# The first and the last iterations of a pipelined graph-network kernel written out by hand, engine by engine

## The chip, the cores and the metric

The kernel runs on 1 core of one Trainium2 chip. The metric is the device time of one execution in microseconds (us); lower is better. The time before is the median of 3 runs.

## The reference

128 graphs of 128 nodes, 256 features each, pass through four layers; after each one the layer's result is added to its input and the row is normalised. All of it is float32.

```python
H = (adj != 0);  w = adj[:, 0, :]
# L0: two hypergraph convolutions, relu and layer norm between them
xw = x @ W1.T;  Dn = 1 / (H @ w);  Be = 1 / H.sum(axis=1)
h = relu(Dn * (H @ (Be * (H.T @ xw))) + b1)
h = layer_norm(h) * gamma + beta
y = Dn * (H @ (Be * (H.T @ (h @ W2.T)))) + b2 + x
x = norm(x + y)                                                   # n1 -> x1
# L1: mean aggregation
x = norm(x + relu(concat([x, adj @ x / max(adj.sum(-1), 1e-6)]) @ W.T))   # n2 -> x2
# L2: three graph convolutions
g = relu(adj @ (x @ V1) + c1);  g = relu(adj @ (g @ V2) + c2)
x = norm(x + adj @ (g @ V3) + c3)                                 # n3 -> x3
# L3: one convolution, with rows masked that are zero throughout
out = relu((adj @ x) @ K) * (any(x != 0))
x = norm(x + out)                                                 # n4 -> x4
```

## The kernel before, in words

Two graphs make a pair, and there are 64 pairs. The work of a pair is cut into 17 stages on TensorE (PE); `LAG` gives the iteration, counted from the pair's own number, in which each stage runs: G (H times its weighted transpose), Tr (a transpose), Gx in iteration p; R, P, GP in p+1; xT, XAB, AXB in p+2; Ax2, H1, H1W, H2 in p+3; H2W, AP3, Ax3, TK in p+4; the last sum, n4, in p+5. Iteration n so works on five or six pairs at once, and PE runs the stages in the order R G xT H2W Ax2 XAB H1 AP3 P Tr AXB H1W Ax3 Gx H2 GP TK. A product of precision is made of three matmuls, high by high, high by low and low by high: the tiles `*_hi` are rounded copies, made on ScalarE (ACT), and the tiles `*_lo` are the rest, made by a subtraction on VectorE (DVE) where the source lies in PSUM, and on GpSimd (POOL) where it lies in SBUF: `low_r` (r_lo), `low_p` (p_lo), h1 and h2 (both h_lo), `low_GT`, `low_A`.

Each engine has a program of its own, `fill()` and then `body(n)`, and runs it strictly in order; semaphores tie them together. `fill()` holds iterations 0 to 2 and the preparation of the weights: `w2_columns` and `betaW_rows` are two small PE products (psum<-w2g,ones and psum<-n_s,beta_b), from which DVE makes the centred `w2c_hi`, `w2c_lo` and `betaW`. From iteration 3 on `body(n)` is the same to the last iteration, 68, with those stages left out that have no pair (`if active(...)`). Where a stage writes in the 8 PSUM banks is fixed by `BANK`; a stage waits until the one before it in its bank has been read.

The end of a pair (iteration p+5, stage F): ACT takes the relu of TK's product (L846, tk), DVE counts the non-zero elements of x3 (L1151, L1155: mask), POOL multiplies tk by mask (L1321) and adds x3 (L1329: n4.s), DVE takes the moments, ACT the root, DVE the inverse and the shift (L888), ACT writes x4 (L576), and SP stores it.

In the rows matmuls and their tiles are named as the program names them: psum<-gx,w1T is R, psum<-w2c,r is P, psum<-p,GT is GP, psum<-ident,x is xT, psum<-wab,x1T is XAB, psum<-xbw,A is AXB, psum<-A_f,x is Ax2 or Ax3, psum<-ax,v is H1, psum<-v,h is H1W or H2W, psum<-A_f,h1w is H2, psum<-h2w,A is AP3, psum<-wk,ax is TK.

Of the kernel before, what the change touches and what calls it, by code (L numbers as in the profile page):

```python
# [16 lines left out]
LAG = dict(prep=-1, G=0, Tr=0, Gx=0,  # L17
           R=1, P=1, GP=1,
           x1=2, xT=2, XAB=2, AXB=2,
           x2=3, Ax2=3, H1=3, H1W=3, H2=3,  # L20
           H2W=4, AP3=4, Ax3=4, TK=4,
           F=5)


BANK = dict(R=0, Ax2=0, Tr=0, GP=4, H1=1, Gx=1, XAB=2, AXB=2, TK=2, H2=3, xT=4, P=4,
            H2W=6, H1W=6, G=(5, 7), AP3=7, Ax3=7)
# [4 lines left out]
def build(nc, x, adjT, w1T, w2T, wab, v1, v2, v3, wk, columns, rows, eye, out):
# [4 lines left out]
    END = NP + LAG["F"]  # L36

    with ExitStack() as ctx:
# [133 lines left out]
        def first(n, j):  # L172

            return n == j

        def active(stage, n):
            return 0 <= n - LAG[stage] < NP

        def bank(stage, pair):

            if stage == "G" and pair == 2:
                return 6, 7
            if stage == "Tr" and pair in (1, 2):
                return 3 * pair
            if stage == "GP" and pair == 0:
                return 2
            if stage == "xT" and pair == 0:
                return 3
            return BANK[stage]

        def steps(fill, body):

            fill()
            for n in range(FILL, END):
                body(n, n)

        def at_count(p, k):
# [1196 lines left out]
```

## Time and profile before

| | |
|---|---|
| time, median of 3 runs | 1439.89 us (1439.43 to 1441.12) |
| the profiled execution: its own time | 1440.07 us |
| its span, first to last instruction | 1438.3 us |
| PE busy | 1389.8 us, 97% of the span |
| DVE, ACT, POOL busy | 1119.3, 1124.9, 1045.4 us (78%, 78%, 73%) |
| chain of work that ended last | PE 94% |
| mean granted TensorE clock | 0.987 |

The profiled execution lies 0.18 us over the median, and its span 1.77 us under its own time. The busy time of PE counts a matmul from its start to its modelled end; in a row of matmuls without a gap they overlap, and what one costs is the distance from its start to the next one's.

### The profile page before, as it was taken

What the parts mean: (1) busy time and instruction counts of PE and PEld (TensorE: products, weight loads), DVE (VectorE), ACT (ScalarE), POOL (GpSimd) and SP (SyncE); (2) the same over time, 40 slices, a digit from 0 to 9 for tenths busy, and PEclk for the clock granted to TensorE, in tenths of its full rate; (3) what the DMA queues carried; (4) which work ended last, traced back from release to release, by engine and by line L of the source; (5) the groups of instructions that cost most, each with busy time, mean ns of one, the idle gap of its engine ahead of it and who ended that gap; (6) DMA issues with size and microseconds to landing.
All of it is one profiled execution on the core that took longest, in us unless ns stands there. A gap on an engine that the chain in (4) does not pass through costs nothing.

```text
span 1438.3 us, 34672 instructions
## 1 busy us (share of the span) xinstructions
PE 1389.8 (97%) x10896; PEld 1347.0 (94%) x10896; DVE 1119.3 (78%) x4060; ACT 1124.9 (78%) x2634; POOL 1045.4 (73%) x1096
## 2 busy tenths in 40 slices
PE   5899999999999999999999999999999999999974
PEld 5799999999999999999999999999999999999974
DVE  5578888887877878878878888787787787887763
ACT  4578788788788778878878878878877877887853
POOL 4667777877877877777787787787787777777742
PEclk9899999999999999999999999999999999999997
DMA  3001011011011011011101101101101101100000
GB/s 128 22 24 38 19 39 38 20 39 38 20 38 38 20 38 38 27 31 38 33 25 39 38 20 38 38 20 38 39 20 38 39 20 38 39 29 18 16 15 23
DMA packets 29956, 47.13 MB, mean 33 GB/s; under 512 B 3408, under 2 KB 12240, under 8 KB 29776
## 3 DMA queue, kind: packets, MB, share of 16 engines
q1 hardware_dynamic: 29776, 44.91, 10.0%
q8 instruction: 90, 1.47, 0.4%
q14 instruction: 90, 0.74, 0.2%
HBM read 28.12 MB, written 16.78 MB: 31 GB/s over the span
## 4 chain that ended last, share of the span: by engine, by line
PE 94%; DVE 2%; issue 1%; ACT 1%; POOL 0%; DMA 0%; POOLq 0%; ACTq 0%; DVEq 0%
PE psum L265 91%; PE psum L384 2%; PE psum L313 1%; DVE n_st L866 1%; DVE p_f L1009 0%; ACT x L576 0%; DVE n_s L1039 0%; DVE n_s L1178 0%; DVE psum L1029 0%; DMA at_in<-adjT 0%; ACT n_std L571 0%; DVE x L898 0%; DVE w2g L1095 0%; ACT h_f L581 0%; DVE psum L871 0%
## 5 line engine op out<-in xcount | busy, mean ns | idle before, releaser
L576 ACT ACTIVATE x<-n_s,n_shift,n_rstd 128x256 f32<-128x256 f32 x384 | 208.8, 592 | 1.2 <-DVE n_shift L888 0.9
L1229 POOL TENSOR_TENSOR h_lo<-h_f,h_hi 128x512 fp32r<-128x512 f32 x128 | 164.1, 1282 | 55.4 <-ACT h_hi L557 55.4
L1237 POOL TENSOR_TENSOR r_lo<-r_f,r_hi 128x512 fp32r<-128x512 f32 x128 | 164.6, 1288 | 52.7 <-ACT r_hi L557 45.9
L1321 POOL TENSOR_TENSOR n_s<-tk,mask 128x512 f32<-128x512 f32 x64 | 66.7, 1042 | 154.8 <-DVE mask L1155 141.3
L265 PE MATMUL psum<-v_hi,h_hi 128*128 128x256 f32 x512 | 150.5, 294 | 5.8 <-issue 4.5
L866 DVE BATCH_NORM_STATS2 n_st<-n_s 128x6 f32<-128x256 f32 x384 | 141.9, 411 | 7.5 <-POOL n_s L1329 5.2
L265 PE MATMUL psum<-w2c_hi,r_hi 128*128 128x258 f32 x512 | 147.2, 287 | 0.0
L265 PE MATMUL psum<-w2c_lo,r_hi 128*128 128x258 f32 x512 | 145.9, 285 | 0.0
L265 PE MATMUL psum<-v_hi,h_lo 128*128 128x256 f32 x512 | 145.2, 284 | 0.0
L265 PE MATMUL psum<-w2c_hi,r_lo 128*128 128x258 f32 x512 | 145.1, 283 | 0.0
L265 PE MATMUL psum<-v_lo,h_hi 128*128 128x256 f32 x512 | 144.9, 283 | 0.0
L265 PE MATMUL psum<-gx_hi,w1T_hi 128*128 128x256 f32 x512 | 144.3, 282 | 0.0
L265 PE MATMUL psum<-A_f,x 128*128 128x128 f32 x1024 | 138.8, 280 | 5.2 <-ACT x L576 4.4
L265 PE MATMUL psum<-gx_hi,w1T_lo 128*128 128x256 f32 x512 | 143.7, 281 | 0.0
L265 PE MATMUL psum<-gx_lo,w1T_hi 128*128 128x256 f32 x512 | 143.6, 280 | 0.0
L581 ACT ACTIVATE h_f<-psum,columns 128x256 f32<-128x256 f32 x256 | 107.3, 471 | 44.9 <-PE psum L265 44.9
L571 ACT ACTIVATE n_std<-psum,eps_c 128x2 f32<-128x2 f32 x192 | 49.2, 256 | 116.8 <-DVE psum L871 116.8
L265 PEld LDWEIGHTS psum<-A_f,x 128*128 128x128 f32 x1024 | 128.4, 196 | 5.8 <-ACT x L576 4.8
L1229 POOL TENSOR_TENSOR p_lo<-p_f,p_hi 128x512 fp32r<-128x512 f32 x64 | 81.9, 1280 | 63.9 <-ACT p_hi L557 63.9
L855 DVE TENSOR_TENSOR ax_lo<-psum,ax_hi 128x512 fp32r<-128x512 f32 x128 | 88.6, 692 | 33.7 <-ACT ax_hi L557 29.5
L855 DVE TENSOR_TENSOR x1T_lo<-psum,x1T_hi 128x512 fp32r<-128x512 f32 x64 | 44.3, 692 | 81.8 <-ACT x1T_hi L557 81.8
L265 PE MATMUL psum<-wab_hi,x1T_hi 128*128 128x512 f32 x256 | 107.5, 420 | 0.0
(158 smaller groups left out, 5426.2 us busy)
## 6 DMA issues: line engine op xcount, KB each, us to landing
x_in<-x_in_dram SPq DMA_DIRECT2D x64, 256.0 KB, 2.8
out<-x SPq DMA_DIRECT2D x64, 256.0 KB, 2.0
at_in<-adjT SPq DMA_DIRECT2D x64, 128.0 KB, 2.2
x<-v_in SPq DMA_DIRECT2D x3, 256.0 KB, 5.1
n_s<-w2T_in SPq DMA_DIRECT2D x2, 256.0 KB, 3.8
r_f<-w1T_in SPq DMA_DIRECT2D x2, 256.0 KB, 4.7
h_f<-wab_in SPq DMA_DIRECT2D x2, 256.0 KB, 5.9
rows<-rows_in SPq DMA_DIRECT2D x1, 256.0 KB, 6.2
```

The costliest lines, as they stand in the source:

```text
L265: return pe.matmul(o, a, b, start=start, stop=stop)
L313: last = pe.transpose(psum[:, bank("Tr", p), cols(g)], Gd[:, g, :], ident[:])
L384: last = pe.transpose(psum[:, bank("xT", p), (2 * m + g) * C:(2 * m + g + 1) * C], x1[:, g, cols(m)], ident[:])
L571: act.activation(nm.std[:], nm.mv[:, :, 1], ACT.Sqrt, bias=eps_c[:, 0:1]).then_inc(nm.rooted, 1)
L576: last = act.activation(dst[:, g, :], nm.s[:, g, :], ACT.Identity, scale=nm.rstd[:, g:g + 1], bias=nm.shift[:, g:g + 1])
L581: return act.activation(dst[:, m].rearrange("p g c -> p (g c)"), psum[:, BANK[stage] + extra, (m % 2) * 2 * C:(m % 2 + 1) * 2 * C], ACT.Re ...
L855: return dve.tensor_tensor(dst[1][:], src, f(dst[0][:]), ALU.subtract).then_inc(signal, 1)
L866: last = dve.bn_stats(nm.st[:, g, :], sum_n1_psum(p, g) if nm is n1 else nm.s[:, g, :])
L1229: return pool.tensor_tensor(dst[1][:], src, f(dst[0][:]), ALU.subtract).then_inc(signal, 1)
L1237: pool.tensor_tensor(r_s[1][:, half], r_f[:, half], f(r_s[0][:, half]), ALU.subtract).then_inc(r_lo[h], 1)
L1321: pool.tensor_tensor(n4.s[:], tk[:], bc(mask[:], [C, 2, D], 2), ALU.mult).then_inc(tk_masked, 1)
```

## The change

The diff rewrites every engine's program. The functions of single steps (`R`, `low_gx`, `invert`, and so on) keep their instructions and take the pair's number alone. What differs:

1. Iterations 0 to 5 (`fill()`) and 63 to 68 (`drain()`) are lists of steps in an order of their own for each engine. The iterations in between, 6 to 62, keep the order that they had on every engine.
2. In these lists a stage may write in any bank: `BANK_OF` gives it, and the waits that keep a bank from being overwritten stand in the lists. R is split in its halves `R0` and `R1`, P in `P(p, 0)`, `P(p, 1)` and `squares(p)`.
3. In the lists a step of SBUF sources (`low_r`, `low_p`, `low_A`, `low_h1`, `low_h2`, `low_v`, `low_w1`, `low_wab`, `add_squares`, `sum_squares`, `make_xb`, `sum_n4`) may run on DVE or POOL. In fill 14 of POOL's steps stand on DVE and 3 of DVE's on POOL; in drain 16 of POOL's stand on DVE.
4. For pairs 60 to 63 (`MASKED`) the mask is the scale of the relu on ACT, one instruction for each graph, and `sum_n4` adds tk and x3 in one instruction. The multiplication on POOL is gone for them.
5. x1 has two buffers; the moments of n2, n3 and n4 lie in SBUF outside the middle iterations; the order of the loads is the one before, and each of the late weights has a semaphore of its own.
6. In the middle iterations the waits differ a little: PE has 55 in an iteration instead of 54, DVE 72 instead of 63, ACT 69 instead of 65, POOL 31 instead of 25.

```diff
+BANK_OF = {
+    ('G', 0): (6, 7), ('BW', 0): 0, ('Tr', 0): 1, ('Gx', 0): 2, ('W2', 0): 3, ('R0', 0): 4, ('G', 1): (6, 7),
...
+FIRST, LAST = 6, 63
+MASKED = 60
...
+        def sum_n4(e, p):
+            if p >= MASKED:
+                e.wait_ge(tk_relu, upto(p))
+                e.wait_ge(n4.done, upto(p - 1))
+                e.tensor_tensor(n4.s[:], tk[:], x3[:], ALU.add).then_inc(n4.summed, 1)
...
+            def fill():
+                G(0)
+                betaW_rows()
+                Tr(0)
+                Gx(0)
+                w2_columns()
+                R(0, 0)
+                pe.wait_ge(gd_made, 1)
+                G(1)
+                R(0, 1)
...
+                pe.wait_ge(w2_mean, 1)
+                P(0, 0)
+                pe.wait_ge(r_relu[0], 1)
+                pe.wait_ge(r_relu[1], 1)
+                G(2)
+                pe.wait_ge(gd_made, 2)
+                R(1, 0)
+                P(0, 1)
+                squares(0)
+                Tr(2)
...
+                R(1, 1)
...
+                Gx(2)
...
+                G(3)
+                pe.wait_ge(p_made, 1)
+                P(1, 0)
+                Tr(3)
+                P(1, 1)
+                squares(1)
+                pe.wait_ge(r_relu[1], 2)
+                GP(0)
...
+                H1(1)
+                AP3(0)
+                pe.wait_ge(h2_relu, 1)
+                H1W(1)
+                pe.wait_ge(ax2_lo, 2)
+                Ax3(0)
+                pe.wait_ge(n2.summed, 3)
+                H2(1)
+                TK(0)
...
+                AXB(63)
+                pe.wait_ge(h1_relu, 62)
+                H2(61)
+                pe.wait_ge(ax3_lo, 60)
+                H1(62)
+                pe.wait_ge(h2w_lo, 61)
+                TK(59)
+                pe.wait_ge(ax2_lo, 63)
+                H2W(61)
+                pe.wait_ge(h1w_out, 62)
+                H1W(62)
+                pe.wait_ge(n3.summed, 61)
+                Ax2(63)
...
+                H2(63)
+                pe.wait_ge(ax3_lo, 61)
+                AP3(62)
+                pe.wait_ge(h2_relu, 63)
+                TK(61)
+                pe.wait_ge(h1_relu, 64)
+                H2W(63)
+                pe.wait_ge(tk_relu, 61)
+                Ax3(62)
+                pe.wait_ge(h2w_lo, 63)
+                AP3(63)
+                pe.wait_ge(h1w_out, 64)
+                TK(62)
+                pe.wait_ge(ax3_lo, 62)
+                Ax3(63)
+                pe.wait_ge(n3.summed, 63)
+                TK(63)
...
+                    act.wait_ge(mask_made, upto(p))
+                    for g in range(2):
+                        last = act.activation(tk[:, g, :], psum[:, b, g * D:(g + 1) * D], ACT.Relu,
+                                              scale=mask[:, g:g + 1])
```

The start of PE's program before; the rows from gx on are R of pair 0:

```order
L265 MATMUL psum<-BH,HT 128x258 x2
L313 MATMUL psum<-ident,Gd 128x128 x2
L265 MATMUL psum<-GT,x_in 128x128 x4
L265 MATMUL psum<-w2g,ones 128x256 x4
L265 MATMUL psum<-gx_hi,w1T_hi 128x256
```

The same place of the change:

```order
L366 MATMUL psum<-BH,HT 128x258 x2
L366 MATMUL psum<-n_s,beta_b 128x256 x4
L406 MATMUL psum<-ident,Gd 128x128 x2
L366 MATMUL psum<-GT,x_in 128x128 x4
L366 MATMUL psum<-w2g,ones 128x256 x4
L366 MATMUL psum<-gx_hi,w1T_hi 128x256
```

The product for `betaW` (n_s is the buffer that w2T is loaded in) now stands between G and Tr of pair 0; before it followed P of pair 0.

POOL before, at the first p_lo, for whose end PE's GP of pair 0 waits; the BH rows are `make_BH` of pair 2:

```order
L1254 TENSOR_TENSOR BH<-at_in,BH 128x2
L1257 TENSOR_TENSOR be_rest<-be_inv,be_r 128x2
L1260 TENSOR_TENSOR BH<-HT,be_r 128x2x128
L1262 TENSOR_TENSOR BH<-HT,be_rest 128x2x128
L1285 TENSOR_TENSOR xb<-x_in,b2half 128x512
L1229 TENSOR_TENSOR p_lo<-p_f,p_hi 128x512
L1229 TENSOR_TENSOR GT_lo<-GT,GT_hi 128x256
```

POOL in the change, at the same p_lo:

```order
L202 TENSOR_TENSOR v_lo<-x,v_hi 128x512
L202 TENSOR_TENSOR wk_lo<-tk,wk_hi 128x512
L209 TENSOR_TENSOR r_lo<-r_f,r_hi 128x512
L202 TENSOR_TENSOR p_lo<-p_f,p_hi 128x512
L1860 TENSOR_TENSOR BH<-at_in,BH 128x2
```

xb, BH of pair 2 and GT_lo of pairs 0 and 1 no longer stand in front of or behind it; the low part of r of pair 1 (its second half) does, and the weights' low parts.

The end of DVE's program in the change; x is x3, tk the relu's result. In the program before no row n_s<-tk,x stood on DVE; POOL had n_s<-tk,mask and n_s<-n_s,x:

```order
L1448 TENSOR_SCALAR mask<-nz_count 128x2
L1391 RECIPROCAL n_rstd<-n_std 128x2
L1395 SCALAR_TENSOR_TENSOR n_shift<-n_mv,n_rstd 128x2
L202 TENSOR_TENSOR ax_lo<-psum,ax_hi 128x512
L254 TENSOR_TENSOR n_s<-tk,x 128x512
L1371 BN_STATS n_st<-n_s 128x6 x2
```

The sum of the last pair is one instruction on DVE, directly ahead of the moments that need it.

## Rows read from the trace of the kernel before

**Rows 1.** The page's head: the span, and PE's busy time.

```profile
span 1438.3 us, 34672 instructions
PE 1389.8 (97%) x10896; PEld 1347.0 (94%) x10896; DVE 1119.3 (78%) x4060; ACT 1124.9 (78%) x2634; POOL 1045.4 (73%) x1096
```

**Rows 2.** Windows: length; busy time (instructions) of each engine; granted clock; DMA share; GB/s.

```profile
0.00:97.05 97.05, 75.72 (x492) 69.69 (x493) 60.83 (x194) 52.24 (x125) 57.76 (x71) 0.93 0.20 64
17.72:54.86 37.14, 28.38 (x174) 25.89 (x172) 22.50 (x67) 17.34 (x43) 23.23 (x26) 0.86 0.08 22
97.05:118.38 21.33, 21.33 (x173) 20.77 (x171) 17.27 (x64) 16.81 (x40) 16.22 (x18) 1.00 0.00 1
118.38:1334.38 1216.00, 1216.00 (x9692) 1184.32 (x9691) 984.75 (x3593) 995.12 (x2338) 925.13 (x970) 1.00 0.11 32
1334.38:1438.30 103.92, 76.74 (x546) 72.19 (x544) 56.45 (x213) 60.69 (x133) 46.28 (x40) 0.88 0.05 19
1396.94:1438.30 41.36, 19.19 (x116) 17.60 (x116) 13.73 (x59) 16.41 (x35) 11.94 (x10) 0.75 0.07 26
```

**Rows 3.** Timeline of PE: start, duration; matmuls in a row without a gap.

```profile
1350.72 0.28 PE L265 MATMUL psum<-v_hi,h_lo 128*128 128x256 f32 x1
1350.83 1.05 PE L265 MATMUL psum<-A_f,x 128*128 128x128 f32 x8
1351.72 0.50 PE L265 MATMUL psum<-GT,x_in 128*128 128x128 f32 x3
...
1362.23 0.39 PE L265 MATMUL psum<-wab_lo,x1T_hi 128*128 128x512 f32 x1
1362.46 0.40 PE L265 MATMUL psum<-wab_hi,x1T_lo 128*128 128x512 f32 x1
```

**Rows 4.** Timeline of PE in the fill; in brackets the idle time ahead of the instruction.

```profile
5.65 0.80 PE L265 MATMUL psum<-BH,HT 128*128 128x258 f32 x2 [5.65 <-POOL BH L1262]
8.50 0.66 PE L313 MATMUL psum<-ident,Gd 128*128 128x128 f32 x2 [2.04 <-DVE Gd L945]
...
35.98 0.55 PE L265 MATMUL psum<-p_hi,GT_hi 128*128 128x256 f32 x1 [4.41 <-issue]
...
57.70 0.66 PE L384 MATMUL psum<-ident,x 128*128 128x128 f32 x4 [2.60 <-DVE x L898]
```

**Rows 5.** Timeline of DVE and POOL: the same POOL operation with and without DVE's.

```profile
15.55 1.49 DVE L1095 TENSOR_TENSOR w2g<-w2g,w2mean 128x1024 f32<-128x1024 f32 x1
...
15.92 1.72 POOL L1229 TENSOR_TENSOR GT_lo<-GT,GT_hi 128x256 fp32r<-128x256 f32 x1
35.84 0.72 POOL L1229 TENSOR_TENSOR GT_lo<-GT,GT_hi 128x256 fp32r<-128x256 f32 x1
```

**Rows 6.** Timeline of the last iterations: what PE waited for.

```profile
1414.96 0.36 PE L265 MATMUL psum<-v_hi,h_hi 128*128 128x256 f32 x1 [0.79 <-issue]
1418.09 0.36 PE L265 MATMUL psum<-h2w_hi,A_hi 128*128 128x256 f32 x1 [1.46 <-ACT h2w_hi L557]
1423.20 2.08 PE L265 MATMUL psum<-A_f,x 128*128 128x128 f32 x8 [4.16 <-ACT x L576]
```

**Rows 7.** Timeline of ACT, POOL and DVE behind the last matmul.

```profile
1429.68 0.60 ACT L846 ACTIVATE tk<-psum 128x512 f32<-128x512 f32 x1 [2.79 <-PE psum L265]
...
1430.35 1.04 POOL L1321 TENSOR_TENSOR n_s<-tk,mask 128x512 f32<-128x512 f32 x1 [12.93 <-ACT tk L846]
1431.47 1.26 POOL L1329 TENSOR_TENSOR n_s<-n_s,x 128x512 f32<-128x512 f32 x1
...
1432.76 0.75 DVE L866 BATCH_NORM_STATS2 n_st<-n_s 128x6 f32<-128x256 f32 x2 [5.25 <-POOL n_s L1329]
```

**Rows 8.** The page's groups: busy us, mean ns of one, idle before.

```profile
L1229 POOL TENSOR_TENSOR h_lo<-h_f,h_hi 128x512 fp32r<-128x512 f32 x128 | 164.1, 1282 | 55.4 <-ACT h_hi L557 55.4
...
L581 ACT ACTIVATE h_f<-psum,columns 128x256 f32<-128x256 f32 x256 | 107.3, 471 | 44.9 <-PE psum L265 44.9
...
L855 DVE TENSOR_TENSOR x1T_lo<-psum,x1T_hi 128x512 fp32r<-128x512 f32 x64 | 44.3, 692 | 81.8 <-ACT x1T_hi L557 81.8
```

More of the change, by code:

```diff
@@ L14 @@
 TINY = 1.1754944e-38
[L17 to L26, printed above, removed]
-BANKS = 8
-FILL = 3
+BANK = dict(R0=1, R1=0, Ax2=0, Tr=0, GP=4, H1=1, Gx=1, XAB=2, AXB=2, TK=2, H2=3, xT=4, P=4,
+            H2W=6, H1W=6, G=(5, 7), AP3=7, Ax3=7, W2=2, BW=3)
+BANKS = 8
+BANK_OF = {
[14 rows of a table added]
+}
+FIRST, LAST = 6, 63
+MASKED = 60
 def build(nc, x, adjT, w1T, w2T, wab, v1, v2, v3, wk, columns, rows, eye, out):
@@ L170, in upto, with inputs @@
             return min(pair, NP - 1) + 1
[L172 to L177, printed above, removed]
         def bank(stage, pair):
[L181 to L197, printed above, removed]
+            return BANK_OF.get((stage, pair), BANK[stage])
+        def inputs(p):
             return 16 * (p // RING + 1)
@@ L256, in _, with body @@
+                load_v(3)
+                load_at(3)
+                load_x(3)
+                reload(4)
+                reload(5)
+                reload(6)
+                reload(7)
+                store(0)
+            def body(n):
+                if n + 2 < NP:
+                    reload(n + 2)
+                store(n - 5)
+            fill()
+            for n in range(FIRST, NP + 5):
+                body(n)
             for j in range(2):
@@ L360, in P, with squares @@
+                last.then_inc(pe_did[f"R{h}"], 1)
+            def P(p, h):
+                if p == 0 and h == 0:
+                    pe.wait_ge(w2c_lo, 1)
+                pe.wait_ge(r_lo[h], upto(p))
+                for g in range(2):
+                    product(psum[:, bank("P", p) + g, 0:D + 2],
+                            [(part(r_s, ALL, m, g), part(w2c_s, ALL, m)) for m in (2 * h, 2 * h + 1)],
+                            start=h == 0, stop=h == 1)
+            def squares(p):
                 pe.wait_ge(sq_sum, upto(p))
@@ L554, in _ @@
+            fill()
+            for n in range(FIRST, LAST):
+                body(n)
+            drain()
         @block.scalar
@@ L639, in round_p, with high_x1T, high_h2w, high_ax2 @@
+            def high_x1T(p):
+                high("xT", x1T, x1T_hi, p, pe_did["XAB"])
+            def high_h2w(p):
+                high("H2W", h2w, h2w_hi, p, pe_did["AP3"])
+            def high_ax2(p):
+                high("Ax2", ax2, ax2_hi, p, pe_did["H1"])
+            def high_ax3(p):
+                high("Ax3", ax3, ax3_hi, p, pe_did["TK"])
+            def round_p(p):
                 act.wait_ge(p_made, upto(p))
@@ L1223, in _ @@
-            steps(fill, body)
+                prep(0)
+                spread_beta()
+                scale_G(0)
+                scale_w2()
+                prep(1)
+                copy_betaW()
+                low_w1(dve, 1)
+                low_gx(0)
+                halve_b2()
+                mean_w2()
+                make_xb(dve, 0)
+                centre_w2()
+                prep(2)
+                scale_G(1)
+                low_w2()
+                low_r(dve, 0, 1)
+                add_squares(dve, 0)
@@ L1354 @@
+            fill()
+            for n in range(FIRST, LAST):
+                body(n)
+            drain()
 def kernel(x, adj, L0_gnn_W1, L0_gnn_b1, L0_gnn_gamma, L0_gnn_beta, L0_gnn_W2, L0_gnn_b2, L1_gnn_W,
```

2041 lines of the change are left out of this document (1264 added, 777 removed), and 13 rows, old and new, of the table BANK_OF.

## The prediction

> **What bounds the kernel now.** I read the page's head first: PE is busy for 1389.8 of 1438.3 us, the other engines for 73 to 78% [rows 1]. Then the windows, to see where PE is not busy. Iterations 6 to 62 fill 118.38 to 1334.38 us; PE is busy for all of it at full clock, so an iteration costs 1216.00 / 57 = 21.33 us and nothing but matmuls sets it [rows 2]. All loss lies outside. A pair's matmuls are one iteration's, so 64 pairs need 64 x 21.33 = 1365.3 us, and the two weight products about 3.2 (an estimate: 8 float32 matmuls of 256 columns, each twice the 0.22 that one of 128 costs below). That makes 1368.5; the span is 1438.3; 69.8 us are lost.
>
> To split them, I need the work left at 1334.38, where iteration 63 begins. The distance between starts in the timeline is 0.12 us for a matmul of 256 columns, 0.23 for 512, and 0.89 for four float32 matmuls of 128 columns (1350.83 to 1351.72; the trace counts each as two) [rows 3]. By these R costs 2.84, P 3.23, XAB 2.89, each of H1, H1W, H2W, TK 1.40 to 1.52, AP3, AXB, GP about 0.78, Ax2, Ax3, Gx, H2 about 0.87, xT 0.36, G 0.24, Tr 0.17, together 21.33. Left over at 1334.38 are G, Tr, Gx of one pair, R, P, GP of two, xT, XAB, AXB of three, Ax2, H1, H1W, H2 of four, H2W, AP3, Ax3, TK of five: 68.1 us of work, which take 103.9 to the end. **The drain loses 35.8.** The rest, 34.0, is lost in the fill, before iteration 5 starts at 97.05 (63.1 us of work in 97.05). In both stretches the granted clock is also down: 0.86 in 17.72 to 54.86, 0.75 behind 1396.94 [rows 2]; the low of the two levels is 1.2 GHz, and it follows stretches in which PE stood idle.
>
> What PE waits for is latency: one pair's chain, with nothing else in PE's queue that may run. In the fill these are the first G (5.65), Gd (2.04), p_lo (4.41, a wait for POOL under the name of issue, since p_lo stands behind the BH and xb work there) and x1 (2.60) [rows 4].
>
> **The change part by part.** The middle is untouched: same order, 57 iterations, 57 x 21.33. PE gets one more wait in an iteration, DVE nine. PE now stands before 54 waits an iteration and still shows no gap [rows 2], so the waits of semaphores long reached cost it nothing; DVE has 21.33 - 17.27 = 4.1 us idle in an iteration, which covers nine waits unless each costs 0.45. I take 0, and up to 0.05 us an iteration (3 us) for the range.
>
> *Fill.* I followed the new lists by hand, each step with its duration from the trace and the waits that the code names.
> - Up to 22 us little can be won. w2c_lo, which P of pair 0 needs, hangs on a chain of loads, gx, W2's product, centring on DVE. betaW's product, now ahead of Tr of pair 0, waits for w2T and takes Tr from 8.50 to about 10.3, but it also brings the full clock earlier, and it is gone from behind P(0). R(0) starts at 14.5 (before 14.61), P(0) at 22.3 (22.16).
> - From there on R, G, Gx and P of pairs 1 to 3 stand between. P(0) ends at 28.4, GP(0) at 36.3 with P(1), G(2), G(3), Gx(2) done: 5.0 us of work more and 1.3 us earlier than before, so 6.3 ahead. The 4.41 wait is filled.
> - DVE then sets the pace for a while. XAB(0) ends at 46.1, AXB(0) at 51.6 (waits for xbw_lo), H1(0) at 62.8, Ax2(1) at 70.5. Small stalls follow for pair 1's h1_lo (2.3), x3(0) and h1w (0.8). TK(0) ends at 83.6, where R(4) starts, which is 97.05 before: 13.4 ahead.
> - Such a list is too smooth; each dip of PE's clock costs, as the 37 us at 0.86 before did. I take off 1.4: **12.0**.
>
> *Drain.* The work without any stall puts H2 of pair 63 (behind which 9.8 us of work stand) at 1334.38 + 68.1 - 9.8 = 1392.7. By hand the stalls are 0.75 (low_r of pair 62, since DVE runs 2 us behind), 0.5, 0.5, 0.55 up to AXB(63) at 1378.3, and then 0.4, 0.4, 0.35: 3.4 in all, H2(63) at 1396.1. H2W(63) follows at 1400.7 (relu, rounding, low part on POOL, with pair 61's x4 ahead of the relu). Before it started at 1414.96 [rows 6]. From there the chain of the last pair is the bound, with or without the change: matmuls, 1.46, 4.16 and 1.46 us of waiting for the other engines (1.46 twice, ahead of AP3 and of TK), and 8.7 behind the last matmul, in all 1438.3 - 1414.96 = 23.3 [rows 6].
> - The mask is the one step of it that is shortened. Behind tk's relu (ends 1430.28) POOL needs until 1432.73 for two instructions, 2.5 us [rows 7]. Now ACT's relu is two instructions (2 x 0.47 at most, against one of 0.60, so up to 0.3 more [rows 8]), and the sum takes DVE 0.69 [rows 8] instead of POOL's 1.26. The step costs about 1.0: 1.45 saved. The end is at 1400.7 + 23.3 - 1.45 = 1422.6, so the drain wins 15.7. I take off 0.7 for clock: **15.0**.
>
> Sum: 12.0 + 15.0 + 0 = 27.0. The profiled execution took 1440.07; less 27.0 that is 1413.1. It lies 0.18 over the median of 1439.89, so I say 1413.
>
> *Steps moved between POOL and DVE.* A low part of 512 elements costs POOL 1282 ns and DVE 692 [rows 8]; 30 steps go to DVE. In the drain DVE has 56.45 us of work [rows 2] and gets 16 steps of at most 0.69, about 10 more: 66 in some 88 us, fine as a mean. Up to H1W(63) its list adds up to 49.5 us against 54 us of PE's work, so it is close, and that is where my stalls come from. There is a price on the other side: GT_lo took POOL 1.72 us at 15.92, while DVE worked on two SBUF operands (15.55 to 17.04), and 0.72 at 35.84 [rows 5]; POOL stood still for about the time of DVE's instruction. All the moved low parts are of this kind. The Trainium skill, GPSIMD Engine Reference, section 1 (Specifications), says that POOL's SBUF interfaces are shared with VectorE, with contention when DVE has two SBUF inputs; the trace agrees.
>
> **The rivals.**
> - *A: POOL held up by DVE.* If each of the 30 moved steps (20 us of DVE time) holds up a POOL instruction and half of these lie on the chain, 10 us come back: 1423. For it: the row of 1.72. Against: POOL has only 46 us of work in 104 us of the drain [rows 2] and less after the change, so most steps meet it idle. Half of the effect is likelier than the whole; 1418 to 1423. Chance 0.15. (This is the skill's rule above taken at its full price.)
> - *B: better than my list.* The lists fit so well that stalls are about 2 us in the drain, and the fill keeps PE busy from 22 us on. Floor: the fill loses 13.7 us up to 22.3 and nothing after, R(4) at 76.8, 20.3 ahead; the drain, without stalls and with the last chain, wins 19.1. That is 1400.6. Halfway to it is 1407. Chance 0.2.
> - *C: little gained, the clock.* In a denser but still broken stretch PE stays at 1.2 GHz. The fill has 63 us of work; if 20 us of it run at half the clock, 10 are lost, and in the drain 5: 1428. For it: 0.86 and 0.75 now [rows 2], with idle times no longer than 4.4. Against: the idle times before which the clock fell are those being filled. Chance 0.08.
> - *D: slower.* The middle loses its freedom from gaps: an iteration's nine more waits on DVE land on one of its chains (x1 or n2), which PE awaits each time. From 27.0 / 57 = 0.47 us an iteration the gain is eaten, above it the kernel is slower; at 0.6 it is 1413 + 34 = 1447. For it: DVE is the busiest of the three. Against: 4.1 us idle an iteration, 0.05 us for each wait needed. Chance 0.02.
> - *E: no change*, because the stalls only move: an engine in front (DVE's 49.5 us) sets the drain's length, and the fill is bound by the weights' chain further than 22 us. Both gains would have to vanish. Chance 0.02.
>
> **How the numbers follow.** My forecast, 1409 to 1418, has 0.53. With B (0.2), A (0.15) and C (0.08) at their values, 1404 leaves out the better half of B (0.08), and 1424 leaves out C, D and E (0.12). The range is 1404 to 1424. A measurement of this kernel can tell 0.2%, 2.9 us, from no change: faster means under 1437. Of the cases A, B, C and the forecast are faster: 0.96; E is the same, 0.02; D slower, 0.02.
>
> **What would show it.** Iterations 6 to 62 at 21.33 with PE busy throughout; if D holds, idle time of PE there, released by DVE. In the fill: R(4), the stage in front of pair 5's G, at 84 to 87 us; a granted clock over 0.9 between 22 and 50; the product for betaW between 7.3 and 10.4, Tr behind it. In the drain: H2W(63) 64 to 69 us behind the start of iteration 63's work, then about 22 to the end; behind the last matmul 7.2 us instead of 8.7, with no POOL in it. If A holds, POOL's low parts take 1.5 to 2 us in fill and drain, and PE waits for them. What would make the prediction wrong is above all my hand-made list: it takes all durations from a calm queue, and gives each of PE's waits only the one partner that comes last by it.

## The result, and the profile after

The changed kernel takes 1420.15 us (median of 4 runs, 1419.96 to 1421.42), the kernel before beside it 1439.66 us (1439.27 to 1441.12): ratio 0.9865, 95% interval 0.985 to 0.9881. It is faster by 19.5 us where 27 were forecast: inside the range, above the 1409 to 1418 of the forecast itself, and in the stretch that was given to rival A.

The profiled execution took 1421.42 us, the slowest of the four, with a span of 1419.6, 18.7 less than before [rows 1]. The page's head of the changed kernel:

```profile
span 1419.6 us, 35305 instructions
PE 1385.0 (98%) x10896; PEld 1340.8 (94%) x10896; DVE 1141.7 (80%) x4086; ACT 1128.1 (79%) x2639; POOL 1013.5 (71%) x1065
```

Windows of the changed kernel, cut at the same stages as [rows 2]: up to R(4); iteration 5; iterations 6 to 62; from R(62), where iteration 63 begins, to the end; from H2W(63) to the end (length; busy time and instructions of each engine; granted clock; DMA share; GB/s).

```profile
0.00:90.97 90.97, 73.36 (x493) 66.93 (x493) 70.70 (x209) 54.47 (x127) 48.33 (x60) 0.96 0.21 68
90.97:112.78 21.81, 21.76 (x173) 20.95 (x171) 17.22 (x59) 16.83 (x39) 15.29 (x17) 1.00 0.00 2
112.78:1329.04 1216.26, 1215.98 (x9692) 1183.88 (x9691) 985.91 (x3593) 996.02 (x2338) 925.59 (x970) 1.00 0.10 32
1329.04:1419.60 90.56, 73.87 (x546) 69.06 (x544) 67.83 (x230) 60.81 (x137) 24.30 (x20) 0.94 0.06 21
1396.52:1419.60 23.08, 10.34 (x58) 9.10 (x58) 11.42 (x47) 9.54 (x21) 0.00 (x0) 0.77 0.09 34
```

Set against [rows 2]: up to R(4) 97.05 has become 90.97 (6.1 won), iteration 5 takes 21.81 instead of 21.33 (0.5 lost), the middle 1216.26 instead of 1216.00 (0.3 lost), the drain 90.56 instead of 103.92 (13.4 won). 6.1 - 0.5 - 0.3 + 13.4 = 18.7. The drain was forecast at 15.0, the fill at 12.0 and gave half of that.

PE's timeline in the fill of the changed kernel (start, duration, in brackets the idle time ahead):

```profile
6.35 0.58 PE L366 MATMUL psum<-BH,HT 128*128 128x258 f32 x1 [6.35 <-POOL BH L1868]
...
7.43 0.79 PE L366 MATMUL psum<-n_s,beta_b 128*128 128x256 f32 x1 [0.28 <-DMA n_s<-w2T_in]
...
22.95 0.30 PE L406 MATMUL psum<-ident,Gd 128*128 128x128 f32 x1 [4.38 <-DVE Gd L1470]
...
25.59 0.56 PE L366 MATMUL psum<-w2c_hi,r_hi 128*128 128x258 f32 x1
...
40.34 0.37 PE L366 MATMUL psum<-p_hi,GT_hi 128*128 128x256 f32 x1
...
84.03 0.36 PE L366 MATMUL psum<-v_hi,h_hi 128*128 128x256 f32 x1 [2.20 <-POOL h_lo L202]
```

G(0) starts at 6.35 (5.65 in [rows 4]), the first P at 25.59 (forecast 22.3), GP(0) at 40.34 (35.98 in [rows 4]) and ends at 41.30 (forecast 36.3), so here the new fill is behind the old one, with more work done; R(4) is at 90.97 (forecast 83.6). Before the first P stands a wait of 4.38 us for Gd(1), which DVE makes. DVE's and POOL's timelines at two places ahead of it:

```profile
3.67 0.62 DVE L1483 TENSOR_SCALAR be<-ht_count 128x2 f32<-128x2 f32 x1
...
16.65 2.31 DVE L1571 TENSOR_TENSOR w2g<-w2g,w2mean 128x1024 f32<-128x1024 f32 x1
18.89 0.81 DVE L1479 TENSOR_SCALAR HT<-at_in 128x256 fp32r<-128x256 f32 x1
...
3.54 0.72 POOL L202 TENSOR_TENSOR A_lo<-at_in,A_hi 128x256 fp32r<-128x256 f32 x1 [3.10 <-ACT A_hi L853]
...
16.15 1.74 POOL L271 TENSOR_TENSOR wab_lo<-h_f,wab_hi 128x512 fp32r<-128x512 f32 x1
17.84 1.71 POOL L202 TENSOR_TENSOR GT_lo<-GT,GT_hi 128x256 fp32r<-128x256 f32 x1
```

`be`, two columns wide, took 0.17 us in every iteration of before (168 to 172 ns, 64 times). Here it takes 0.62 and ends at 4.29, just behind POOL's A_lo (4.26), which now stands ahead of BH(0). The w2g subtraction took 1.49 us [rows 5] and takes 2.31 beside wab_lo and GT_lo; HT 0.81, where the one at 2.89 took 0.29. [rows 5] showed POOL held up by DVE; here DVE is held up by POOL, and from gx_lo at 14.42 until Gd(1) is done at 22.8 us DVE has no idle time.

### The profile page after: what moved, and what is told of

Read it like the earlier page. It is cut to its first block, busy times and chain, and to the rows that moved or that the text cites. A ratio compares the mean times of both kernels' runs of the same rounds, so it can differ in the third digit from the quotient of the medians.

```text
span 1419.6 us, 35305 instructions
## 1 busy us (share of the span) xinstructions
PE 1385.0 (98%) x10896; PEld 1340.8 (94%) x10896; DVE 1141.7 (80%) x4086; ACT 1128.1 (79%) x2639; POOL 1013.5 (71%) x1065
## 4 chain that ended last, share of the span: by engine, by line
PE 93%; DVE 4%; issue 1%; ACT 1%; DMA 0%; SPq 0%; POOL 0%; ACTq 0%; DVEq 0%
PE psum L366 90%; PE psum L452 2%; PE psum L406 1%; DVE n_st L1371 1%; DMA n_s<-w2T_in 0%; ACT x L872 0%; DVE x L1409 0%; ACT h_hi L853 0%; DVE sq L221 0%; ACT h_f L877 0%; ACT tk L1034 0%; DVE be L1483 0%; DVE Gd L1470 0%; DVE Gl L1466 0%; DVE n_shift L1395 0%
## 5 line engine op out<-in xcount | busy, mean ns | idle before, releaser
L202 POOL TENSOR_TENSOR h_lo<-h_f,h_hi 128x512 fp32r<-128x512 f32 x123 | 159.1, 1293 | 60.3 <-ACT h_hi L853 60.3
L209 POOL TENSOR_TENSOR r_lo<-r_f,r_hi 128x512 fp32r<-128x512 f32 x122 | 157.1, 1288 | 44.9 <-ACT r_hi L853 39.3
L1890 POOL TENSOR_TENSOR n_s<-tk,mask 128x512 f32<-128x512 f32 x60 | 62.7, 1045 | 145.5 <-DVE mask L1448 144.7
L867 ACT ACTIVATE n_std<-psum,eps_c 128x2 f32<-128x2 f32 x171 | 43.9, 257 | 97.5 <-DVE psum L1380 97.5
L202 POOL TENSOR_TENSOR p_lo<-p_f,p_hi 128x512 fp32r<-128x512 f32 x61 | 78.3, 1284 | 56.4 <-ACT p_hi L853 56.4
L877 ACT ACTIVATE r_f<-psum,columns 128x256 f32<-128x256 f32 x256 | 100.5, 469 | 5.2 <-PE psum L366 5.0
```

The lines of the kernel that those rows point to most:

```text
L202: return e.tensor_tensor(dst[1][:], src, f(dst[0][:]), ALU.subtract).then_inc(signal, 1)
L209: e.tensor_tensor(r_s[1][:, half], r_f[:, half], f(r_s[0][:, half]), ALU.subtract).then_inc(r_lo[h], 1)
L867: act.activation(nm.std[:], nm.mv(p)[:, :, 1], ACT.Sqrt, bias=eps_c[:, 0:1]).then_inc(nm.rooted, 1)
L877: return act.activation(dst[:, m].rearrange("p g c -> p (g c)"), psum[:, bank(stage, p), (m % 2) * 2 * C:(m % 2 + 1) * 2 * C], ACT.Relu, b ...
L1890: pool.tensor_tensor(n4.s[:], tk[:], bc(mask[:], [C, 2, D], 2), ALU.mult).then_inc(tk_masked, 1)
```

## The experiments

A theory came out of the traces. Theory 1: the fill is short of its forecast because DVE's instructions wait for POOL's. Rival: something else in the fill is the bound, namely the betaW product ahead of Tr(0), or the pace of PE behind the first P. Ratios are to runs of the kernel before on the same chip: 1440.21 us (9 runs) beside e1 to e4, 1441.09 (6) beside c1, e5, e6 and e8, 1439.79 (9) beside e9 to e11 and the last.

**Fill alone, drain alone.** e1_fill_alone keeps the new fill and runs iterations 63 to 68 in the order of before; e2_drain_alone the reverse.

```diff
@@ e1_fill_alone
-FIRST, LAST = 6, 63
-MASKED = 60
+FIRST, LAST = 6, 69
+MASKED = 64
@@ e2_drain_alone
-FIRST, LAST = 6, 63
+FIRST, LAST = 3, 63
```

> The new fill alone; iterations 63 to 68 in the order, the banks and the engines of the kernel before, mask on POOL. By the trace of the change the fill is worth 5.6 us (R of pair 4 starts at 90.97 instead of 97.05, and the iteration behind it takes 21.8 instead of 21.3). If the two ends are independent: 1439.7 - 5.6 = 1434. If the fill had worked as predicted, it would be 1428.

> The new drain alone; iterations 0 to 5 in the order, the banks and the engines of the kernel before. By the trace of the change the drain takes 90.6 us instead of 103.9: 1439.7 - 13.4 = 1426. If the middle pays for the changed waits, the two gains of this run and of the fill alone add up to more than 19.5; if not, to 19.5 within 1.

Measured: e1 1434.71 us (0.9957, 0.9943 to 0.9971), e2 1427.03 (0.9909, 0.9895 to 0.9923), that is 5.5 and 13.2 us under before. Together 18.7, within 1 us of the 19.5 of both at once. The two parts are independent; the fill falls 6.5 us short of its forecast, the drain 1.8.

**The mask on POOL again**, the relu in one instruction, all else as changed.

```diff
-MASKED = 60
+MASKED = 64
@@ gpsimd, drain()
+                mask_tk(60)
...
+                mask_tk(63)
```

> The change, with the mask of pairs 60 to 63 as POOL's multiplication again. If the prediction's sum for the step is right, the time behind the last matmul grows from 7.1 to 8.2 or 8.5 us and the kernel by 1.1 to 1.5: 1421.4. If the mask in the relu was worth nothing, 1420.2.

Measured 1425.0 us (0.9894, 0.988 to 0.9907), 4.9 over the changed kernel's median; in the profiled execution, the fastest of four, the drain takes 94.20 us instead of 90.56, 3.6 more. Behind the last matmul it is 8.01 instead of 7.11, 0.9. The other 2.7 lie ahead, and DVE's timeline of this kernel shows where:

```profile
1396.85 0.69 DVE L257 TENSOR_TENSOR n_s<-n_s,x 128x512 f32<-128x512 f32 x1 [1.96 <-POOL n_s L1890]
...
1405.22 0.69 DVE L257 TENSOR_TENSOR n_s<-n_s,x 128x512 f32<-128x512 f32 x1 [1.70 <-POOL n_s L1890]
```

DVE's queue stands at the sum of pairs 61 and 62 until POOL has multiplied; behind it stand n3's inverse and shift for the next pair, so Ax3(61), Ax3(62) and Ax3(63) wait 1.10, 1.53 and 4.10 us for x3 instead of 0.32, 0.35 and 3.22. In this order of DVE's queue the mask in the relu is worth more than twice the 1.45 us that I gave it.

**The drain's low parts on POOL again.** All 16 steps moved back to POOL, each where it ran by time.

```diff
-                low_r(dve, 62, 0)
...
-                low_p(dve, 62)
-                low_p(dve, 63)
...
-                sum_n4(dve, 63)
+                low_r(pool, 62, 0)
...
+                sum_n4(pool, 63)
```

> The change, with the 16 steps of the drain that went to DVE back on POOL, each at the place where it ran by time. Theory 1, speed of the engine: a step on the last pairs' chain costs 0.6 us more on POOL; seven or so lie on it, so 3 to 5 us: 1424. Rival, shared access: since DVE and POOL hold each other up, it hardly matters who does the step, and POOL's being free takes load off DVE: within 1.5 of 1420.

Measured 1424.04 us (0.9889, 0.9875 to 0.9902); the drain takes 94.92, 4.4 more than the changed kernel's. p_lo on POOL costs PE 1.9 us of waits instead of 0.9. A third of the drain's 13.4 us is the choice of engine, in this order of the lists.

**The changed kernel again.**

> The changed kernel once more, as the yardstick for the three runs beside it. Both theories: 1420 us, and a fill whose iteration 5 begins between 109.5 and 113, since the same fill has differed by that much between executions.

Measured 1420.41 us (0.9857, 0.984 to 0.9875). The same lists: R(0) 14.32 (15.26 in the first trace), first P 24.78 (25.59), GP(0) 39.35 (40.34), R(4) 89.91 (90.97), drain 90.56 again. The start of the fill differs by 1 us between these two executions; the load of w2T lands at different times (PE takes it up at 6.93 and at 7.43). Five more of the kernels here have the changed fill as it is (e1, e3, e4, e10 and m1). In the seven traces the first P lies at 24.32 to 25.71, but always 10.3 to 10.6 us behind R(0); R(4) lies at 88.03 (e4) to 90.97. So an effect on the first P is read from R(0) on, and a difference of less than 3 us at R(4) between two single traces shows nothing.

**POOL quiet while DVE is on the chain.** wab_lo stood at 16.15 and 19.51 us; it takes the places of v_lo, which moves back.

```diff
@@ gpsimd, fill()
-                low_A(pool, 0)
                 make_BH(0)
-                low_w1(pool, 0)
+                low_A(pool, 0)
...
-                low_wab(pool, 0)
...
-                low_wab(pool, 1)
...
-                low_v(pool, 0)
+                low_wab(pool, 0)
...
@@ vector, fill()
+                low_w1(dve, 0)
```

> The changed kernel with GpSimd kept quiet while VectorE is on the chain of the fill: A_lo(0) behind BH(0), both halves of w1T_lo on VectorE, both wab_lo moved from 16.1 and 19.5 us to where the first v_lo stood, the v_lo behind them later. Theory 1 (the fill is short of its forecast because VectorE's instructions last longer while a GpSimd instruction runs): G(0) at 5.65 instead of 6.35 us, the w2g subtraction 1.1 to 1.5 us instead of 2.31, the first P at 22 to 23.5 us instead of 25.59, and the kernel 2 to 3 us faster, near 1417.5. Rival (the fill is bound by when w2T lands and by the betaW product ahead of Tr(0), and the long VectorE instructions only fill waits): G(0) earlier, but the first P later than 24.5, and the kernel within 1 us of 1420.

Measured 1419.4 us (0.9856, 0.9838 to 0.9873). `be` 0.17, G(0) at 5.89, the w2g subtraction 1.76, R(0) to first P 9.64 us instead of 10.33 and 10.46; first P at 24.17, R(4) at 89.42. DVE is faster as the theory says, but R(4) is only 0.5 us earlier than in the run beside it, which the spread of the same fill covers, and the times can't be told apart. Other instructions of DVE still meet POOL (`be` of pair 2 takes 0.80). The theory's direction holds; its size, 3 us of the kernel, does not.

**The head of POOL's queue alone**: that diff down to `low_w1(pool, 0)` and A_lo behind it, and its last line.

> The changed kernel with only the head of GpSimd's queue changed: A_lo(0) behind BH(0) instead of ahead of it, and both halves of w1T_lo on VectorE; the two wab_lo stay at 16.1 and 19.5 us. Theory 1: `be` of iteration 0 takes 0.17 us again instead of 0.62, G(0) at 5.65, the four w2g scalings 1.1 to 1.3 us instead of 2.06; of the 3 us by which the first P is late some 0.7 come back (24.6 to 25.1), the rest staying with the two wab_lo; the kernel 0 to 1 us faster, near 1419.5. Rival: no different from the changed kernel at the first P.

Measured 1418.88 us (0.9852, 0.9836 to 0.9867). `be` takes 0.17 and the four w2g scalings 1.13 us (2.06 before), as expected; R(0) is at 14.93, the first P at 25.26, R(4) at 90.33, none of them earlier than in the run beside it. G(0) wins 0.55, but the betaW product waits for w2T anyway, so nothing of it reaches P: the rival is right here. The 1.5 us by which the kernel's median is lower are not shown to come from the edit. In the profiled execution iteration 6 starts later than in c1 (112.20 against 111.62); iterations 6 to 62 take 1214.79 us (1216.32 in c1) and the drain 89.61 (90.56), and the edit touches neither. In this drain the eight matmuls of Ax3(63) took 1.13 us, in the first trace of the changed kernel 2.05. The windows of 2.2 us from their start, here and in the changed kernel (the granted clock is the number behind POOL's):

```profile
1404.00:1406.20 2.20, 1.13 (x8) 0.94 (x8) 1.46 (x8) 1.07 (x4) 0.00 (x0) 0.82 0.00 0
```

```profile
1406.05:1408.25 2.20, 2.04 (x8) 1.75 (x8) 1.06 (x7) 0.16 (x2) 0.00 (x0) 0.50 0.00 0
```

**betaW's product behind R(0)**, with its bank, its copy on DVE behind Gd(1), and P's wait moved to match.

```diff
                 G(0)
-                betaW_rows()
...
                 R(0, 1)
+                pe.wait_ge(w2_mean, 1)
+                betaW_rows()
```

> The changed kernel with the betaW product, on which Tr(0) waits from 8.5 to 11.0 us, moved behind R(0), into the idle time ahead of Tr(1), with its copy behind Gd(1). Theory 1 (VectorE held up by GpSimd): Tr(0) at about 9.1 and R(0) at about 13.4 instead of 15.26, but the first P depends on Gd(1) and w2c, whose VectorE instructions stay where they are behind w2g: the first P at 24.5 to 25.5, the kernel within 1 us of 1420. Rival (the product ahead of Tr(0) sets the fill): the first P at 23.5 or earlier, and 1.5 to 2 us faster, 1418 to 1418.5.

Measured 1419.56 us (0.9856, 0.984 to 0.9871). Tr(0) is at 9.26 instead of 10.34 (c1), but R(0) at 15.14, not at 13.4. PE's timeline of this kernel:

```profile
9.26 0.66 PE L406 MATMUL psum<-ident,Gd 128*128 128x128 f32 x2 [2.04 <-DVE Gd L1470]
10.39 2.08 PE L366 MATMUL psum<-GT,x_in 128*128 128x128 f32 x8 [0.47 <-ACT GT L853]
12.26 3.23 PE L366 MATMUL psum<-w2g,ones 128*128 128x256 f32 x8
15.14 0.47 PE L366 MATMUL psum<-gx_hi,w1T_hi 128*128 128x256 f32 x1
```

The W2 product takes 3.23 us here and 1.89 where the betaW product has kept PE busy ahead of it (3.50 at 11.55 in the kernel before). So the product ahead of Tr(0) pays for itself by PE's pace, as forecast; the profile gives a granted clock of 1.00 in both stretches, so that the clock makes the difference is not shown. The first P is at 24.66, where c1 has 24.78, since Tr(1) waits for Gd(1) until 22.81 all the same: that rival falls.

**Gd(1) first.**

```diff
                 centre_w2()
-                prep(2)
                 scale_G(1)
+                prep(2)
```

> The changed kernel with one exchange in VectorE's fill: the five instructions that make G of pair 1 into Gd stand ahead of the three that prepare pair 2, instead of behind them. The part of theory 1 under test: P(0) is late because Tr(1) waits 4.4 us for Gd(1), which VectorE's queue, drawn out by GpSimd, reaches late. Expected: Tr(1) at 20.5 to 21.3 instead of 22.95 us, the first P bound by w2c_lo then, at 24.0 to 24.6 instead of 25.59, the kernel 1 to 1.5 us faster, near 1419. Rival (VectorE's whole queue, not the place of Gd(1) in it, is what P hangs on): the first P as before and the kernel unchanged.

Measured 1420.82 us (0.987, 0.9856 to 0.9883): nothing won, and R(0) to first P takes 10.72. DVE's, ACT's and PE's timelines of this kernel:

```profile
20.52 0.61 DVE L1470 SCALAR_TENSOR_TENSOR Gd<-psum,dinv,Gl 128x128 f32<-128x128 f32 x2
...
22.51 0.17 DVE L1487 RECIPROCAL be_inv<-be 128x2 f32<-128x2 f32 x1
...
22.71 0.20 ACT L853 ACTIVATE be_r<-be_inv 128x2 fp32r<-128x2 f32 x1 [2.26 <-DVE be_inv L1487]
...
24.21 0.36 ACT L853 ACTIVATE GT<-psum 128x256 f32<-128x256 f32 x1
...
24.67 0.55 PE L366 MATMUL psum<-GT,x_in 128*128 128x128 f32 x1 [2.99 <-issue]
```

Tr(1) runs at 21.27 as expected, but ACT's queue stands until pair 2's be_inv, now later, and behind it wait r's second relu and the copy of GT(1). Gx(1) starts at 24.67 and P behind it. The rival is right that the place of Gd(1) alone wins nothing: the exchange moves the wait into ACT's queue.

**The last chain.**

```diff
@@ scalar, drain()
-                relu_tk(62)
                 root(n3, 63)
+                relu_tk(62)
@@ gpsimd, drain()
-                low_h2(pool, 63)
@@ vector, drain()
+                low_h2(dve, 63)
                 sum_n4(dve, 61)
...
+                low_h2w(63)
                 count_nonzero(62)
-                low_h2w(63)
...
+                invert_shift(n3, 63)
                 sum_n4(dve, 62)
-                invert_shift(n3, 63)
```

> The changed kernel with four exchanges in the last chain: the square root of n3 of pair 63 on ScalarE ahead of tk's relu of pair 62 (and its shift on VectorE ahead of pair 62's sum), h2w_lo(63) ahead of the count for pair 62's mask, and h2_lo(63) on VectorE instead of GpSimd. Theory (the drain is 1.2 us short of its forecast behind H2W(63) because pair 62's steps stand ahead of pair 63's, and its h2_lo costs 1.26 us on GpSimd against 0.69): H2W(63) 66.9 instead of 67.5 us behind the start of iteration 63's work, the last matmul 81.7 to 82.0 instead of 83.45, the drain 88.8 to 89.2 instead of 90.56, the kernel 1.5 us faster, near 1418.7. Rival (the last chain's waits are latencies of the engines that no order changes): within 0.5 us of the changed kernel's drain.

Measured 1420.95 us (1417.68 to 1421.14; 0.9864, 0.9851 to 0.9878), the drain 90.60: nothing. H2W(63) starts 0.45 earlier, as expected (67.03 us behind R(62)), but Ax3(63) at 77.05 us, before at 77.01. DVE's, ACT's and PE's timelines of this kernel:

```profile
1402.62 0.16 DVE L1395 SCALAR_TENSOR_TENSOR n_shift<-n_mv,n_rstd 128x2 f32<-128x2 f32 x1
1403.14 0.69 DVE L254 TENSOR_TENSOR n_s<-tk,x 128x512 f32<-128x512 f32 x1 [0.37 <-ACT tk L1034]
...
1403.92 1.09 ACT L872 ACTIVATE x<-n_s,n_shift,n_rstd 128x256 f32<-128x256 f32 x2 [0.81 <-DVE n_s L254]
...
1405.15 0.55 PE L366 MATMUL psum<-A_f,x 128*128 128x128 f32 x1 [2.98 <-ACT x L872]
```

In the changed kernel the same chain of pair 63 has, on PE:

```profile
1396.52 0.36 PE L366 MATMUL psum<-v_hi,h_hi 128*128 128x256 f32 x1 [1.44 <-POOL h_lo L202]
...
1400.15 0.36 PE L366 MATMUL psum<-h2w_hi,A_hi 128*128 128x256 f32 x1 [0.47 <-DVE h2w_lo L202]
...
1406.05 2.05 PE L366 MATMUL psum<-A_f,x 128*128 128x128 f32 x8 [3.22 <-ACT x L872]
```

In e10 the shift is ready at 1402.78, and still ACT writes x3(63) only at 1403.92, behind DVE's sum for pair 62. x3 has one buffer (`make_x3` waits for `n4.summed` of the pair before), and that sum needs TK(62), which my exchange made wait 0.80 us for ax_lo(62). The drain packs the last pairs so tightly that pair 62's end is on pair 63's chain. A second buffer of x3 wasn't tried.

**All edits at once**, with h1_lo(1) on DVE too.

```diff
-                low_h1(pool, 1)
...
                 sum_n3(0)
+                low_h1(dve, 1)
```

> All edits at once: GpSimd quiet at the head of the fill and wab_lo later, the betaW product behind R(0), Gd(1) first, h1_lo(1) on VectorE, and the four exchanges of the last chain. If each keeps its own effect: the first P at 21.5 to 22.5 us, GP(0) at 36 to 37.5 (forecast 36.3, changed kernel 40.34), iteration 5 at 107.5 to 109.5, the drain at 89, the kernel at 1414 to 1416. Rival (the stages behind the first P are bound by VectorE's later queue, so an earlier P only waits longer): GP(0) earlier, but R(4) within 1 us of the changed kernel's, and the kernel at 1418.

Measured 1417.59 us (5 runs, 1417.58 to 1418.18; 0.9847, 0.9834 to 0.986), 3.2 and 3.4 us under e9 and e10, which ran beside it. All five times lie below the eight of the changed kernel and c1 (1418.34 to 1421.42), so it beats both kernels; the 1414 to 1416 expected were missed. PE's timeline of it, and its window from the first P to R(4), with that of the changed kernel's first trace behind it:

```profile
22.47 0.37 PE L366 MATMUL psum<-w2c_hi,r_hi 128*128 128x258 f32 x1
...
38.09 0.37 PE L366 MATMUL psum<-p_hi,GT_hi 128*128 128x256 f32 x1
```

```profile
22.47:88.86 66.39, 59.41 (x432) 55.08 (x430) 53.56 (x156) 41.82 (x99) 35.72 (x40) 0.97 0.07 19
```

```profile
25.59:90.97 65.38, 59.77 (x431) 55.58 (x430) 51.06 (x156) 42.00 (x98) 33.30 (x37) 0.96 0.07 19
```

The first P is at 22.47, where I had walked it (22.3), 3.1 us ahead of the changed kernel's, but by luck in part: R(0) comes at 13.66 (walked 14.5; in this execution the W2 product took 2.28 us, in e6 with the same place for betaW 3.23), and from there to the first P it is 8.81 us, where the walk had 7.8 and the changed kernel 10.33. R(4) is 2.1 ahead of the first trace and 1.05 ahead of c1's, and 0.8 behind e4's, which has the unedited fill. From the first P to R(4) it is 66.39 us, in the seven traces of the changed fill 63.71 to 65.38. R(5), where iteration 6 starts (the expectation calls it iteration 5), is at 110.46, not by 109.5. Behind the first P the rival is right: part of what is won there is waited for again. The drain, with the lists of e10, takes 89.74 us instead of 90.60, and Ax3(63) 1.13 us instead of 2.04, so part of this trace's gain is again PE's pace. Which of the edits make the 3 us isn't separated.

**DVE beside POOL, measured by itself.** Behind the changed kernel's last instruction DVE runs seven forms alone, and again beside twelve POOL instructions.

```diff
+            for i in range(3):
+                dve.tensor_scalar(small[:, 0, 8 * i:8 * i + 2], nz_count[:], 1.0, None, ALU.max)
+            for i in range(3):
+                dve.tensor_scalar(sq_[:, i], x3[:, 0], 0.5, None, ALU.mult)
...
+            for i, dst in enumerate(dsts):
+                t = pool.tensor_tensor(dst, tk[:], x3[:], ALU.subtract)
```

> The changed kernel with a measurement behind its last instruction: VectorE runs seven forms of instruction two or three times each, first alone, then beside twelve GpSimd tensor_tensor of 128x512 with three SBUF operands. Theory 1 (VectorE waits for a running GpSimd instruction, in some forms only): alone every form as in the rows of before (0.17, 0.28, 0.69, 0.41, 0.17, 0.42 us); beside GpSimd the tensor_scalar with SBUF operands, which ran at two columns a cycle, rise to 0.6 us and above, and so does the tensor_tensor with two SBUF operands; reads of PSUM, the reciprocal and the reduction stay. Rival (the long instructions of the fill have another cause, such as DMA traffic or the late arrival of an operand): no form is longer beside GpSimd by more than 10%. GpSimd's tensor_tensor: 1.28 us beside forms that stay, up to 1.9 beside the others.

Groups of its last 22 us (shapes, count, busy us, mean ns; Gl, sq, p_f and xa are written alone, Gd, w2g and x beside POOL):

```profile
L2020 POOL TENSOR_TENSOR v_lo<-tk,x 128x512 fp32r<-128x512 f32 x3 | 3.9, 1315 | 0.0
...
L1866 DVE TENSOR_TENSOR x<-tk,x 128x512 f32<-128x512 f32 x2 | 3.4, 1744 | 0.0
L1864 DVE TENSOR_SCALAR w2g<-x 128x256 f32<-128x256 f32 x3 | 2.8, 991 | 0.0
...
L1862 DVE TENSOR_SCALAR Gd<-nz_count 128x2 f32<-128x2 f32 x3 | 2.4, 866 | 1.4 <-POOL v_hi L2020 1.4
L2020 POOL TENSOR_TENSOR wk_lo<-tk,x 128x512 fp32r<-128x512 f32 x1 | 1.7, 1711 | 0.0
...
L1874 DVE TENSOR_REDUCE Gl<-x 128x2 f32<-128x256 f32 x3 | 1.0, 402 | 0.0
L1874 DVE TENSOR_REDUCE Gd<-x 128x2 f32<-128x256 f32 x3 | 1.0, 397 | 0.0
...
L1864 DVE TENSOR_SCALAR sq<-x 128x256 f32<-128x256 f32 x3 | 0.7, 285 | 0.0
L1866 DVE TENSOR_TENSOR p_f<-tk,x 128x512 f32<-128x512 f32 x1 | 0.7, 682 | 0.0
...
L1868 DVE TENSOR_TENSOR xa<-psum,x 128x512 f32<-128x512 f32 x1 | 0.7, 680 | 0.0
L1868 DVE TENSOR_TENSOR x<-psum,x 128x512 f32<-128x512 f32 x1 | 0.7, 679 | 0.0
...
L1862 DVE TENSOR_SCALAR Gl<-nz_count 128x2 f32<-128x2 f32 x3 | 0.3, 164 | 1.3 <-ACT x L873 1.3
L1872 DVE RECIPROCAL Gl<-mask 128x2 f32<-128x2 f32 x3 | 0.3, 143 | 0.0
L1872 DVE RECIPROCAL Gd<-mask 128x2 f32<-128x2 f32 x3 | 0.3, 141 | 0.0
```

Theory 1's mechanism stands: beside POOL a TENSOR_SCALAR from SBUF to SBUF takes 866 ns on the mean instead of 164 with two columns (the first of the three 155, the others 1209 and 1235), 991 instead of 285 with 256 (281, 1346 and 1347); a TENSOR_TENSOR with two SBUF operands 1744 instead of 682, and POOL's 1711 instead of 1260 beside it. With an operand in PSUM it stays (679 and 680), and so do RECIPROCAL (141 and 143) and TENSOR_REDUCE (397 and 402), though both read and write SBUF. It is one execution, and POOL ran one form only.

## Why the prediction was right, and where its terms were off

- **What bounds the kernel, and the middle.** Right: 1216.26 / 57 = 21.34 us an iteration, PE busy in it. Over the traces that keep this middle it takes 1214.79 (e8) to 1216.32 us (c1), before 1216.00, so no price of the added waits shows. D and E fall. Eight matmuls at twice 0.22 are 3.5 us and not 3.2; the 0.3 us are of no weight in the sum.
- **The drain, forecast 15.0, measured 13.4.** The walk gave 15.7, less 0.7 for the clock. H2W(63) starts 67.48 us behind R(62) (walked: 66.3), then 23.08 follow (21.9). The first 1.2 are mostly pace and not waits: at H2(63) the list is 1.0 late (62.74 us against 61.7), though PE idles for 2.5 us up to there and 3.4 were walked; its busy time, 60.22, is 1.9 over the 58.3 of work (68.1 - 9.8). The second 1.2 are a step that failed: I took the last pair's chain as independent of the pair ahead. Before, AP3(63) starts 3.13 us behind H2W(63) and Ax3(63) 8.24; now 3.63 and 9.53. AP3(63) waits 0.47 us for h2w_lo(63), which DVE starts 1.40 us behind the last matmul of H2W(63), before 0.95: x3(62) stands ahead in ACT's queue and pair 62's mask count in DVE's. And x3(63) waits for pair 62's sum (e10). The clock in Ax3(63) alone is worth up to 1 us: with the same lists the drain took 89.61 to 90.61 us.
- **The mask, forecast 1.45.** Behind the last matmul 7.11 us against 8.66, 1.55 won, with no POOL in it, as forecast (7.2). But undone it costs 3.6 us of drain (e3), since I counted only the last pair: the sums of pairs 61 and 62 stand in DVE's queue ahead of x3 of the next pair. It holds for this order of the queue.
- **The fill, forecast 12.0, measured 6.1 up to R(4), 5.6 with iteration 5.** The mis-sized term. Of the 7.4 us between 83.6 (walked) and 90.97, 3.3 lie ahead of the first P: 0.8 ahead of R(0), 2.5 behind it. The step that failed is "R(0) starts at 14.5, P(0) at 22.3": it takes DVE's durations from a calm queue, though the change had put POOL work beside it. From R(0) to the first P the walk has 7.8 us, the changed kernel 10.33; with POOL quieter it is 9.64 (e5), with Gd(1) first alone 10.72 (e9), with all edits 8.81 (e11). So 1.5 of the 2.5 us are shown to lie in POOL's work beside DVE and in the orders of the queues; the cause of the last 1.0 stays open. The other 4.1 lie between first P and R(4), 65.38 us against 61.3 walked: GP(0) ends 5.0 late (41.30 against 36.3), Ax2(1) 5.7 (76.23 against 70.5), R(4) starts 7.4 late. There the list's waits were not too few: by the stage costs worked out from [rows 3] 54.3 us of work stand in it (G, Tr, Gx, R, xT, XAB, AXB of three pairs, P and GP of four, Ax2, H1, H1W, H2 of two, H2W, AP3, Ax3, TK of one), so the walk had 7.0 idle, and the window shows 65.38 - 59.77 = 5.6. PE's busy time is 5.5 over the work: matmuls at less than the full pace, behind each wait. I had taken 1.4 off for that. The granted clock, 0.96 over this window, accounts for about 0.04 x 65.38 = 2.6 of it. In e4's trace of the same fill it was 0.98, and the stretch took 63.71 us; behind the wait of 2.20 us for h1_lo(1) the granted clock was 1.00 there and 0.65 here (84.03 to 88.90), which is 1.2 of the 1.7 us between the two. How the rest divides between the ends that the busy time counts behind each row and slow first matmuls stays open.
- **Rival A.** The time lies in the stretch that A was given (1418 to 1423), and its contention is there, but the sum of A doesn't hold: behind the first G the profile puts only three of PE's waits down to POOL, 2.20 us for h1_lo(1) in the fill (walked 2.3), 0.25 and 1.44 for h_lo in the drain. Single POOL instructions of the fill did last 1.6 to 1.74 us (wab_lo, GT_lo, v_lo, p_lo), as A said; what stood on PE's path was DVE's time, which also grew. The Trainium skill, Trainium Architecture — The Big Picture, section What this means for kernel authors, calls the port pair of DVE and GpSimd "an exclusive lock (not a bandwidth split)". The trace agrees: `be` ends with POOL's instruction (4.29 against 4.26 us), and the side-by-side run shows DVE's TENSOR_SCALAR and TENSOR_TENSOR held up by POOL, and POOL held up by DVE's TENSOR_TENSOR (1711 ns instead of 1260). I had [rows 5] for one direction and didn't ask for the other.
- **Rival C** fell as put (granted clock 0.95 from 17.72 to 54.86, forecast over 0.9), but the clock is part of the 4.1 above. **B** fell. The betaW product stands at 7.43 to 11.0, where 7.3 to 10.4 was walked, and e6 shows that it pays for itself.

## What to carry to other kernels

Before work is moved between VectorE and GpSimd, look at what will run beside it in both directions: here a TENSOR_SCALAR from SBUF to SBUF or a TENSOR_TENSOR with two SBUF operands on VectorE and a TENSOR_TENSOR on GpSimd lasted longer side by side than alone, the short VectorE instruction by up to the length of the GpSimd one; reads of PSUM, RECIPROCAL and TENSOR_REDUCE did not. In a tightly packed end, follow the last pair's chain through every single-buffered tile to the pair ahead; an order changed in one queue mostly moves the wait to the next. When a walk is set against a trace, compare idle time and pace apart, and run the same kernel twice first: here the same fill reached R(4) at 88.03 to 90.97 us in seven traces, a spread wider than what all the edits together gave there.
